# Three transformer layers and a rotation on one core: one pipeline over 96 batches instead of three over 32, with the weights exchanged in place, and an earlier broadcast in the preamble

## The reference, cut to what matters

```python
sh1, sc1, g1, sh2, sc2, g2 = split(silu(c) @ w_mod + b_mod, 6)   # per batch
y = ln(x) * (1 + sc1) + sh1
q, k, v = heads(y @ w_qkv + b_qkv)             # 16 heads of 18
q, k = ln(q) * gq (+ bq), ln(k) * gk (+ bk)    # layers 0 and 2 only
x = x + g1 * (softmax(q k^T / sqrt(18)) v @ w_proj + b_proj)
y = ln(x) * (1 + sc2) + sh2
x = x + g2 * (gelu(y @ w1 + b1) @ w2 + b2)     # w1: 288 x 1152
...
U, _ = qr(P)                                   # after the three layers; P: 288 x 64
R = expm(A)                                    # A: 64 x 64 skew, from W, b and silu(c), per batch
z = x @ U;  x = x + (z @ R - z) @ U^T
```

## Time and profile before

| what | value |
|---|---|
| median of 3 runs | 4670.65 us (4670.15 to 4674.21) |
| the profiled execution's own time | 4671.22 us |
| its span, first to last instruction | 4669.4 us |
| mean granted clock of PE over the span | 0.948 |
| PE busy, share of the span | 4205.1 us, 90% |
| DVE busy | 3631.2 us, 78% |
| ACT busy | 2303.7 us, 49% |
| POOL busy | 1093.6 us, 23% |

### The profile page before, as it was taken

The page is one execution under the profiler, slowest core; times in us unless marked ns, Lnnn a source line. Parts: engine busy times, 40 slices in busy tenths (PEclk is TensorE's granted clock), DMA queues, the critical chain, the costliest instruction groups (busy, mean ns, idle before and its releaser), DMA issues. The chain is left out here.

```text
span 4669.4 us, 124471 instructions
## 1 busy us (share of the span) xinstructions
PE 4205.1 (90%) x46073; PEld 3567.4 (76%) x46073; DVE 3631.2 (78%) x7659; ACT 2303.7 (49%) x3894; POOL 1093.6 (23%) x2045
## 2 busy tenths in 40 slices
PE   6754899999999995999999999975999999999998
PEld 4543688888888874888888888864888888888886
DVE  5665888888988874777777777756888888888884
ACT  1112555555555543555555555534555555555553
POOL 1001222222222222222222222221222222222221
PEclk7576999999999997999999999997999999999999
DMA  3001111110111111111101111011011011110100
GB/s 77 22 0 46 36 28 30 30 30 25 29 30 30 30 30 52 29 30 30 30 24 30 30 30 30 24 38 48 22 29 27 24 31 25 26 27 24 31 24 19
DMA packets 122230, 141.58 MB, mean 30 GB/s; under 512 B 14447, under 2 KB 117781, under 8 KB 122113
## 3 DMA queue, kind: packets, MB, share of 16 engines
q1 hardware_dynamic: 121968, 139.75, 11.3%
q10 hardware_dynamic: 144, 0.22, 0.0%
HBM read 110.87 MB, written 29.06 MB: 30 GB/s over the span
## 5 line engine op out<-in xcount | busy, mean ns | idle before, releaser
L870 DVE TENSOR_REDUCE mx<-S 128x4 f32<-128x1024 f32 x768 | 903.1, 1218 | 180.9 <-PE S L1104 173.4
L630 ACT ACTIVATE pT<-S 128x1024 f32<-128x1024 f32 x768 | 745.4, 1022 | 376.1 <-PE S L1132 375.7
L578 ACT ACTIVATE hf<-M 128x512 f32<-128x512 f32 (+1 forms) x480 | 267.0, 556 | 732.5 <-DVE hl L861 378.7
L507 POOL TENSOR_SCALAR hh<-hf 128x512 fp32r<-128x512 f32 (+1 forms) x480 | 280.3, 584 | 821.9 <-ACT hf L578 783.3
L1132 PE MATMUL S<-qT,kT 32*128 32x256 f32 x9216 | 426.9, 296 | 45.9 <-ACT pT L630 42.5
L1145 PE MATMUL A<-pT,V 128*32 128x256 f32 x6144 | 415.1, 388 | 26.3 <-ACT pT L630 26.3
L1132 PEld LDWEIGHTS S<-qT,kT 32*128 32x128 f32 x9216 | 330.0, 185 | 118.1 <-ACT pT L630 70.4
L1184 PE MATMUL M<-xh,w_hi 128*128 128x256 f32 x1728 | 363.6, 291 | 3.5 <-POOL xh L483 3.5
L1039 PE MATMUL A<-wqkv_hi,xh 128*128 128x288 f32 x1152 | 284.6, 329 | 87.1 <-DVE x L917 79.5
L1223 PE MATMUL M<-w_lo,hh 128*128 128x288 f32 x1728 | 350.5, 304 | 0.0
L1184 PE MATMUL M<-xh,w_lo 128*128 128x256 f32 x1728 | 343.5, 280 | 0.0
(11 more groups left out here) (231 smaller groups left out, 9915.4 us busy)
## 6 DMA issues: line engine op xcount, KB each, us to landing
mid<-xbo SPq DMA_DIRECT2D x64, 288.0 KB, 4.0
xld<-mid SPq DMA_DIRECT2D x64, 288.0 KB, 3.1
xa<-mid SPq DMA_DIRECT2D x64, 288.0 KB, 3.6
gA<-gates SPq DMA_DIRECT2D x96, 144.0 KB, 3.3
gM<-gates SPq DMA_DIRECT2D x96, 144.0 KB, 3.6
xld<-in_x_dram SPq DMA_DIRECT2D x32, 288.0 KB, 3.9
xa<-in_x_dram SPq DMA_DIRECT2D x32, 288.0 KB, 3.5
out_dram<-xbo SPq DMA_DIRECT2D x32, 288.0 KB, 2.2
```

The costliest lines, as they stand in the source:

```text
L507: pool.tensor_scalar(hh[:, 2 * f:2 * f + m, :].rearrange("p m c -> p (m c)"), hf[:, f % 3, 0:m * T], 1.0, 0.0, ALU.mult, ALU.add).then_inc ...
L578: act.activation(hf[:, f % 3, 0:c], MBANK[f % 2][:, 0:c], ACT.Gelu if rot else ACT.Gelu_apprx_tanh).then_inc(s["m_hf"], 1)
L630: act.activation(pT[:, g % 2, 2 * h:2 * h + 2, :], S[:, 2 * h:2 * h + 2, :], ACT.Exp, scale=float(HD) ** -0.5).then_inc(s["a_ex"], 1)
L870: dve.tensor_reduce(mx[:, p, :, :], S[:, r:r + 2, :].rearrange("p a (t k) -> p a t k", t=NT), AX.X, ALU.max).then_inc(s["a_mx"], 1)
```

## The change: what it does

The block per layer goes; one pipeline runs over batches 0 to 95, of which 0 to 31 are layer 0, 32 to 63 layer 1 and 64 to 95 layer 2. Slots around the seams are written out, the others are in a loop per layer. Batch 32 is `nxt` while batch 31 is `p`, 30 `a`, 29 `m` and 28 `d`. The next layer's weights come in eleven chunks through two new staging tiles of 128 x 1152 floats (`wst`): chunks 0 to 2 are `wqkv`, 3 and 4 `wo`, 5 to 7 `w1`, 8 to 10 `w2`, each written over the old weight once its last user in the old layer is through. The place of each step is given by k, the number of slots after that in which the new layer's first batch is `nxt`.

The order of the slots, on every engine:

```diff
+            done = -2
+            for layer in range(LAYERS):
+                now[0] = layer
+                from_, to = layer * B + 3, layer * B + B - 3
+                for a in range(done, from_):
+                    single(a)
+                with eng.Fori(from_, to) as n:
+                    slot(n, n - 1, n - 2, n + 1, n + 2)
+                done = to
+            for a in range(done, LAYERS * B + 2):
+                single(a)
```

The exchange of a chunk: SP loads, ACT makes the high part, POOL the low part (DVE, in `swap_mix`, the mix tensors, with the same two waits):

```diff
+        NSW = 11
+        SW_LOAD = {-1: (0, 1), 0: (2, 3), 1: (4, 5), 2: (6, 7, 8), 3: (9, 10)}
...
+        def swap_load(sp, layer, c):
+            g, to = staged(layer, c)
+            ap = swap_chunks(layer)[c][0]
+            if g >= 2:
+                sp.wait_ge(n_lo, g - 1)
...
+            sp.dma_start(to, ap).then_inc(n_in[g % 2], 16)
...
+            last = layer * B - 1
+            if c <= 2:
+                wait(eng, "a_qkv", last, 6)
+            elif c <= 4:
+                wait(eng, "a_pr", last, 2)
+            elif c <= 7:
+                wait(eng, "m_h", last, 5)
+            else:
+                wait(eng, "m_y", last, 2)
...
+        def swap_high(act, layer, c):
+            g, of = staged(layer, c)
+            act.wait_ge(n_in[g % 2], 16 * (g // 2 + 1))
+            if c <= FULL and QK_EPS[layer] is not None:
+                act.wait_ge(n_mean, c + 1)
+            old_weight(act, layer, c)
+            act.activation(swap_chunks(layer)[c][3][0], of, ACT.Identity).then_inc(n_hi, 1)
...
+            pool.wait_ge(n_hi, g + 1)
+            pool.wait_ge(n_lo, g)
+            pool.tensor_tensor(to[1], of, to[0].bitcast(F32), ALU.subtract).then_inc(n_lo, 1)
```

SP: the chunks of a slot come behind its other loads and its store, and a load of x has one more wait:

```diff
+                if layer_of(n):
+                    wait(sp, "m_out", n - B, 16)
```

POOL's slot (the lines without a plus are there before, too):

```diff
                     A_xh(nxt)
+                swap(nxt, 0, (0,))
...
                     A_v(p)
+                swap(nxt, 0, (1,))
...
                     M_hh(m, 0)
                     M_hh(m, 1)
+                    swap(nxt, 3, (8,))
                     M_residual(m)
                     M_hh(m, 2)
+                    swap(nxt, 3, (9, 10))
                     M_hh(m, 3)
                     M_hh(m, 4)
+                swap(nxt, 1, (3,))
+                swap(nxt, 2, (5, 6))
```

ACT's slot:

```diff
                         A_exp(a, p, i // 2, i % 2)
+                        if i == 1:
+                            swap(nxt, 0, (0,))
+                            swap(nxt, 3, (7,))
+                        if i == 3:
+                            swap(nxt, 0, (1,))
...
                     A_hi(p, 1)
+                swap(nxt, 3, (8,))
...
                     A_ohi(a)
+                swap(nxt, 0, (2,))
+                swap(nxt, 3, (9,))
                     M_gelu(m, 2)
                     M_gelu(m, 3)
+                swap(nxt, 1, (3, 4))
+                swap(nxt, 3, (10,))
                     M_gelu(m, 4)
...
                     A_qkv(nxt, 1)
+                swap(nxt, 2, (5,))
...
                         A_square(nxt)
+                    swap(nxt, 2, (6,))
                     A_qkv(nxt, 4)
```

DVE's slot (`swap_means` is `center` on a staged chunk, and does nothing for layer 1):

```diff
                     A_xl(nxt)
+                swap(nxt, 3, 7)
...
                     A_out(a)
+                swap_means(nxt, 0, (2,))
                     A_lo(p, 0)
...
                     A_olo(a)
+                swap(nxt, 0, 2)
                     M_hl(m, 0)
...
                     M_hl(m, 4)
+                swap(nxt, 1, 4)
                     A_max(p, 6)
                     A_max(p, 7)
                     A_negmax(p)
...
+                swap_means(nxt, -1, (0, 1))
```

PE waits, for a layer's first batch, until 8 chunks are through ahead of the up projection, 5 ahead of the projection, 3 ahead of q, k, v, and all 11 ahead of the down projection:

```diff
+                                new_weights(m, 8)
                         M_up_first(m)
...
+                        new_weights(a, 5)
                     A_proj(a)
...
+                        new_weights(nxt, 3)
                 qkv(0)
...
+                            new_weights(m, NSW)
                         M_down(m, 0, lo, hi)
```

In the preamble, the spread of a round's first step moves from behind item 3 of the products to ahead of the wait for the updates:

```diff
-                        if at == 3 + c * len(work) // len(columns):
+                        if c and at == 3 + c * len(work) // len(columns):
                             spread(j)
...
             for k in range(TAYLOR - 1, 0, -1):
                 i = TAYLOR - k
+                spread(TAYLOR_FROM + sum(Q_TAYLOR[:i - 1]))
                 pe.wait_ge(e_up, 2 * i)
...
             with pe.Fori(0, SQUARINGS) as i:
+                spread(i * Q_SQUARE + SQUARE_FROM)
                 pe.wait_ge(e_up, 2 * i + 2 * TAYLOR)
```

More of the change, by code:

```diff
@@ L128, in build @@
         nmT = sb("nmT", [P, T], F32R)
-        pickf = sb("pickf", [P, QUADS, P])
+        wst = [sb(f"wst{i}", [P, F]) for i in range(2)]
+        pickf = wst[0][:, 0:QUADS * P].rearrange("p (q c) -> p q c", q=QUADS)
         pick = sb("pick", [P, QUADS, P], F32R)
@@ new lines, in build, with layer_of, local, rot @@
+        now = [0]
+        def layer_of(n):
+            return n // B if isinstance(n, int) else now[0]
+        def local(n):
+            return n - layer_of(n) * B
+        def rot(n):
+            return layer_of(n) == LAYERS - 1
+        def eps(n):
+            return QK_EPS[layer_of(n)]
+        def is_first(n):
+            return isinstance(n, int) and n % B == 0
+        def source(n):
+            return t["x"] if layer_of(n) == 0 else mid[layer_of(n) - 1]
+        def target(n):
+            return t["out"] if rot(n) else mid[layer_of(n)]
@@ new lines, in qk_run, with wait_normed, slots, at @@
+        def qk_run(n):
+            return n - B if rot(n) else n
+        def wait_normed(eng, n):
+            if eps(n) is None:
+                wait(eng, "a_qkvd", n, 4)
+            else:
+                wait(eng, "a_nrm", qk_run(n), 1)
+        def slots(eng, slot):
+            def at(n):
+                return n if 0 <= n < LAYERS * B else None
+            def single(a):
+                slot(at(a), at(a - 1), at(a - 2), at(a + 1), at(a + 2))
+            done = -2
[9 more added lines that the diff above has]
+                single(a)
@@ new lines, in swap_center, with seam @@
+        def swap_center(dve, layer, c):
+            g, of = staged(layer, c)
+            dve.wait_ge(n_in[g % 2], 16 * (g // 2 + 1))
+            center(dve, of[:, 0:2 * D], of.shape[0])
+            dve.sem_inc(n_mean, 1)
+        def seam(nxt, k):
+            layer, rest = divmod(nxt - k, B) if isinstance(nxt, int) else (0, 0)
+            return layer if rest == 0 and 0 < layer < LAYERS else None
+        P_FIRST, P_NORMS, P_B2 = 3 * 16, 8 * 16, (3 * 16, 4 * 16, 9 * 16)
+        block = ctx.enter_context(nc.Block())
@@ new lines, in slot @@
+                elif p is not None:
+                    A_xf(nxt, 0)
+                    A_xf(nxt, 1)
+                    A_xf(nxt, 2)
+                if m is not None:
+                    M_xf(m)
+                if a is not None:
+                    load_table(a, 1, gelu(a if m is None else m))
+                if p is not None:
+                    A_hi(p, 0)
+                    A_hi(p, 1)
+                if a is not None and m is None:
+                    high_m(act, 0, range(KC, NCH))
@@ new lines, in slot @@
+                if m is not None:
+                    M_gelu(m, 4)
+                if turns:
+                    R_x(d, 0, nxt)
+                    R_x(d, 1, nxt)
+                if p is not None:
+                    load_table(p, 0, ACT.Exp)
+                if nxt is not None:
+                    if p is None:
+                        act.wait_ge(w_lo, NCH)
+                    A_qkv(nxt, 0)
+                if turns:
+                    R_z(d)
+                if nxt is not None:
+                    A_qkv(nxt, 1)
@@ new lines, in slot, with swap @@
+                swap(nxt, 2, (5,))
+                if turns:
+                    R_y(d)
+                if nxt is not None:
+                    A_qkv(nxt, 2)
+                    A_qkv(nxt, 3)
+                    if eps(nxt) is not None:
+                        A_square(nxt)
+                    swap(nxt, 2, (6,))
+                    A_qkv(nxt, 4)
+                if p is not None:
+                    A_shift(p)
+                if nxt is not None:
+                    A_qkv(nxt, 5)
+            def swap(nxt, k, chunks):
+                layer = seam(nxt, k)
+                if layer is not None:
+                    for c in chunks:
+                        swap_high(act, layer, c)
```

1776 lines of the change are left out of this document (880 added, 896 removed).

## The result

| | before | after |
|---|---|---|
| median of 4 runs | 4670.4 us (4669.64 to 4674.21) | 4508.1 us (4504.82 to 4509.94) |
| ratio, 95% interval | | 0.9649 (0.9637 to 0.9661) |
| the profiled execution: own time, span | 4671.22, 4669.4 us | 4508.88, 4507.2 us |
| mean granted clock of PE | 0.948 | 0.965 |

The forecast was 4497 us, range 4470 to 4540. The time lies in the range, 11 us above the forecast. Those 11 come in the main from the exchange: the low parts that POOL makes hold VectorE up, PE waits longer, and PE's clock falls behind some of the waits.

A forecast was written before the change was run, and what follows sets the result against it. PE sets the pace, DVE close behind; seams drain and fill, DVE's copies wait in the preamble. 4671.2 - 168.7 (seams) - 24 (preamble) + 19 (exchange) = 4497.5, forecast 4497 us, range 4470 to 4540.

The forecast's parts named there:

- The seams give back 168.7 us: Between layers: full slots replace the pipeline's drains and fills, giving back 77.4 and 91.3 us.
- rival (c): DVE's register-computed waits in every slot grow longer, making the kernel slower: 4711 us, chance 0.04.
- The preamble gives 24 us: Preamble basis steps: spreads moved ahead save 32 us of first-copy waits, less 8 given back; bounds 15 to 32.
- The step by which the second spread comes late in half the rounds: Preamble: at PE's lower clock the second spread costs 1.1 us a round; over half the rounds 8 us is given back.
- Rival (b): Preamble: the clock stays low through the rounds, so the early spread gives 15 us, not 24: 4507 us, chance 0.08.
- rival (a): Layer seams: the chunk chain misses its place and PE stands at its waits, 40 us in all: 4538 us, chance 0.15.
- The exchange costs 19 us: Both seams: swapping weights in flight adds 4 + 10 us, plus 5 for POOL beside DVE.
- 4 and 10 for the seams without contention: Exchange work reaching the path: 4 us at the first seam, 10 at the second, before the POOL-beside-DVE price.
- that of POOL beside DVE: Seams: sixteen lows each lengthen one DVE operation by 0.56 us, making 9; half on the path, 5.
- PE's clock stays 1.00: Sign to look for: PE's clock holds at 1.00 from the first layer's start to the end.
- Means: Before layer 2, at k = 0: DVE's mean of chunk 2 adds 1.9 us, those of chunks 0 and 1 0.7.
- The rule that I weighed and did not take: Seams: two-input DVE and reading GpSimd operations exclude each other; would make the 5 us term 10.

The follow-up runs named there:

- e1: Changed kernel with the preamble edit taken back, so a round's first spread again stands behind item 3 of the products: 4534.6 us.
- e6: Changed kernel with all 16 low-part subtractions still on POOL but moved, mostly beside VectorE operations with at most one SBUF input: 4492.42 us.
- e5: Changed kernel without the three subtractions of the mean from layer 2's staged wqkv: 4505.43 us.
- e3: Changed kernel with POOL's 16 low-part subtractions replaced by memsets that take about as long but read nothing: 4490.81 us.
- e8: Changed kernel with each of POOL's 16 low-part subtractions run twice, one behind the other, at its place: 4538.05 us.

## Why the prediction was right, and where it was off

- **The seams give back 168.7 us.** Right: stretches, slot lengths and the first fill and last drain are as taken. Steady slots are unchanged, so rival (c), longer register waits, is out.
- **The preamble gives 24 us.** 25.8 in the trace, 22 to 26.5 by e1. The step by which the second spread comes late in half the rounds left 14 x (0.93 + 0.55) = 20.7 us of second waits; 22.2 - 1.55 = 20.7 are there. Rival (b), 15 us, is out.
- **No new seam.** No wait of PE names a weight, so rival (a) is out; e6 tightened the chain further and PE then waited 0.4 us for a low.
- **The exchange costs 19 us.** It costs 32.0, and this is the mis-sized term. I had 4 and 10 for the seams without contention; with memsets in place of the lows they measure 5.6 and 11.3. The term that failed is that of POOL beside DVE: "Sixteen lows, each lengthening one DVE operation by 0.56, make 9; half of them on the path: 5." The rest, 32.0 - 16.9 = 15.1, is what stands in its place. Two things were wrong in it, and a third was put at nothing. The size: 0.56 came from a 0.4 us copy, and an operation that meets a 2.0 us low loses 1.75 to 1.82 (xl), one that meets low 5 2.5 (hl); VectorE lost 19 us where the term has 9. The share: half was taken to be on the path, and 5.4 to 8.8 of the 19 came through as waits of PE. That 5.4 is near the term's 5 is luck: a size half of the true one met a share that was too large. The clock: 10.2 of the 15.1. "PE's clock stays 1.00" was wrong in both seams, and no term of the sum stands for a fall behind a late input. This is the larger part of the miss.
- **Smaller steps.** Means: 0.7 + 1.9 taken, 6.0 measured by e5 (3.4 of it clock). The mix of chunk 2: 1.1 taken; e3's k = 0 slot at the first seam, 41.49 us, is 1.2 over with all that stands there, and no run takes the mix alone. Most at k = 3: right (5.2 and 8.3), but for hl and x, not for the wait for all 11 chunks.

The rule that I weighed and did not take was right. The Trainium skill (SBUF — State Buffer, Who interferes with whom) has the later of the two wait for the other's end, if the GpSimd operation reads SBUF, and not if it only writes; e3 and the rows of xl agree on both points (2.44 against 0.69). Even by it I had put 10, since I halved twice.

## What to carry to other kernels

Ahead of adding an operation to GpSimd, lay its time over VectorE's line: beside operations with two SBUF inputs it can cost nearly its full length (xl, hl, e8), beside reductions and operations that read PSUM next to nothing (e6), and one wait on a semaphore that VectorE sets anyway moves it from one to the other. When a drain and fill is replaced by an exchange in flight, add up what the exchange does to the busiest two engines' inputs, not only whether its own chain is in time. Where the critical engine is late by a few us, ask what that does to its clock: here it was 11.9 of the 32.0 us.

## What the runs showed of the hardware that was not expected

- The lock works both ways: low 5 above began inside VectorE's hl and took 2.96 us, a low of the same size that begins beside the maxima 2.67.
- A single-input VectorE operation can be shut out too: the negated maxima took 1.86 us beside low 6 of the second seam (0.23 elsewhere), with PE's wait of 2.8 behind it:

```profile
3081.54 2.61 POOL L422 TENSOR_TENSOR w_lo<-wst,w_hi 128x1152 fp32r<-128x1152 f32 x1 [1.82 <-ACT w_hi L415]
...
3082.37 1.86 DVE L1030 TENSOR_SCALAR nm<-mx 128x128 f32<-128x128 f32 x1
```

- After the 3.0 us wait at k = 3, PE's next six matmuls of the down projection took 1.64 us; the same six take 0.96 one slot earlier. So part of the price of a wait comes after it.

```profile
1767.45 0.96 PE L1384 MATMUL M<-w_hi,hh 128*128 128x288 f32 x6
...
1813.64 1.64 PE L1384 MATMUL M<-w_hi,hh 128*128 128x288 f32 x6
```
